# Attention and feed-forward layer on one core: the product of exponentials and values in two visits per group, three score banks, two max banks

## The reference, cut to what matters

```python
x: (16, 512, 128)
qkv = x @ c_attn_w + c_attn_b                       # 16 heads of 8
scores = einsum('bhqd,bhkd->bhqk', q, k) / sqrt(8)  # causal mask, softmax over k
out = einsum('bhqk,bhkd->bhqd', softmax(scores), v)
x = layernorm(x + out @ c_proj_w + c_proj_b)
h = relu(s0 * ([x, -x] @ W0)) * 2                   # 256 -> 512
h = relu(s1 * (h @ W1)) * 2                         # 512 -> 512
x = layernorm(x + s2 * (h @ W2))                    # 512 -> 128
```

## Time and profile before

| | |
|---|---|
| median of three runs | 1046.66 us (1042.14 to 1053.75) |
| the profiled execution's own time | 1043.98 us |
| its span in the profile | 1042.0 us |
| PE busy | 918.4 us, 88% |
| DVE busy | 673.2 us, 65% |
| ACT busy | 605.2 us, 58% |
| POOL busy | 439.5 us, 42% |
| mean granted PE clock | 0.934 of full |

### The profile page before, as it was taken

One profiled execution on the slowest core, in us unless ns is written; L12 is line 12 of the kernel. 1 busy time (PEld: TensorE's weight loads), 2 busy tenths in 40 slices (PEclk: granted clock), 3 DMA queues, 4 the chain that ended last, 5 costly groups with the idle time before them and its releaser, 6 DMA issues.

```text
span 1042.0 us, 20945 instructions
## 1 busy us (share of the span) xinstructions
PE 918.4 (88%) x6848; PEld 505.8 (49%) x6848; DVE 673.2 (65%) x1752; ACT 605.2 (58%) x1106; POOL 439.5 (42%) x505
## 2 busy tenths in 40 slices
PE   2449799999999799988999799998999999999865
PEld 1125345546555355644555355554546555555343
DVE  2346568695858468683776648685695858686334
ACT  2106467575757367573666647674675757566833
POOL 1103244544454345543354434543554454536440
PEclk9657899999999899997999889998999999999997
DMA  3653635354434415353253514534054534400000
GB/s 76 63 66 57 74 51 67 39 76 48 68 57 58 59 23 74 42 74 41 40 73 42 76 32 58 67 47 70 19 74 45 69 45 68 48 22 2 22 10 11
DMA packets 66157, 53.45 MB, mean 51 GB/s; under 512 B 4518, under 2 KB 64006, under 8 KB 66054
## 3 DMA queue, kind: packets, MB, share of 16 engines
q1 hardware_dynamic: 65190, 51.30, 37.4%
q10 hardware_dynamic: 864, 0.79, 0.3%
HBM read 9.24 MB, written 4.19 MB: 13 GB/s over the span
## 4 chain that ended last, share of the span: by engine, by line
PE 58%; ACT 13%; issue 10%; DVE 9%; DMA 5%; SPq 2%; ACTq 2%; POOL 1%; DVEq 0%; POOLq 0%
PE av_ps L899 10%; PE max_ps L840 9%; PE score_ps L866 9%; PE bank_ps L926 7%; PE bank_ps L927 6%; PE bank_ps L823 4%; ACT e L536 4%; ACT res L554 4%; PE max_ps L842 3%; PE bank_ps L972 3%; DMA stack<-parts 2%; DMA stack<-negmaxT 2%; ACT full L528 2%; PE bank_ps L961 2%; SPq L330 2%
## 5 line engine op out<-in xcount | busy, mean ns | idle before, releaser
L536 ACT ACTIVATE e<-score_ps 128x512 f32<-128x512 f32 x640 | 371.3, 598 | 245.2 <-PE score_ps L866 244.3
L840 PE MATMUL max_ps<-stack 72*128 72x512 bf16 (+3 forms) x1024 | 282.0, 315 | 54.7 <-DMA stack<-parts 26.0
L866 PE MATMUL score_ps<-stack 75*128 75x512 bf16 (+3 forms) x1024 | 251.7, 308 | 24.3 <-DMA stack<-negmaxT 15.8
L661 DVE TENSOR_REDUCE negmax<-max_ps 128x1 f32<-128x512 f32 x256 | 170.1, 684 | 155.6 <-PE max_ps L842 132.3
L445 POOL TENSOR_SCALAR_AFFINE_SELECT e<-e 128x512 f32<-128x512 f32 x256 | 164.1, 661 | 168.0 <-ACT e L536 168.0
L840 PEld LDWEIGHTS max_ps<-stack 72*128 72x128 bf16 x1024 | 102.2, 100 | 223.0 <-issue 85.8
L452 POOL TENSOR_TENSOR h_lo<-full,h_hi 128x512 fp32r<-128x512 f32 x120 | 155.3, 1299 | 120.5 <-DVE h_hi L741 119.8
L842 PE MATMUL max_ps<-ident_bf,future_bf 128*128 128x128 bf16 x1024 | 199.6, 227 | 0.0
L899 PE MATMUL av_ps<-e,vaug 128*9 128x512 f32 (+3 forms) x2048 | 193.5, 451 | 1.8 <-ACT avT L543 1.7
L664 DVE TENSOR_REDUCE negmax<-max_ps 128x1 f32<-128x384 f32 x256 | 140.1, 547 | 53.5 <-PE max_ps L842 53.1
L528 ACT ACTIVATE full<-bank_ps,scales 128x512 f32<-128x512 f32 x128 | 86.7, 689 | 101.7 <-PE bank_ps L927 100.0
(11 more groups left out here) (86 smaller groups left out, 950.6 us busy)
## 6 DMA issues: line engine op xcount, KB each, us to landing
stack<-parts SPq DMA_DIRECT2D x288, 128.0 KB
x_in<-in_L_attn_hidden_states SPq DMA_DIRECT2D x16, 256.0 KB, 4.2
x_res<-in_L_attn_hidden_states SPq DMA_DIRECT2D x16, 256.0 KB, 10.2
out_x<-res SPq DMA_DIRECT2D x16, 256.0 KB, 10.0
stack<-negmaxT ACTq DMA_DIRECT2D x32, 24.0 KB
e<-in_L_ffn_k SPq DMA_DIRECT2D x1, 256.0 KB, 3.3
wc<-in_L_attn_c_attn_w SPq DMA_DIRECT2D x1, 192.0 KB
e<-in_L_ffn_k SPq DMA_DIRECT2D x1, 128.0 KB, 3.2
```

What stands on the lines that cost most here:

```text
L536: nc.scalar.activation(e[g % 2][:, t, :], score_ps[:, t % 2, :], ACT.Exp, scale=SCALE).then_inc(exped, 1)
L661: ins = nc.vector.reduce_max(negmax[:, half, 3, h + t:h + t + 1], buf, AX.X, negate=True)
L840: nc.tensor.matmul(out_ap[:, col:col + width], st[0:QK_ROWS, h, 0, P * qt:P * qt + P], st[0:QK_ROWS, h, 1, 0:width], start=True, stop=False)
L866: return nc.tensor.matmul(out_ap[:, col:col + width], st[0:ALL_ROWS, h, 1, P * kt:P * kt + P], st[0:ALL_ROWS, h, 0, P * kt:S], start=True, ...
```

## The change

`SUM_STEPS = (1, 3, 5, 7)` becomes `SUM_STEPS = (2, 6)`: the product is made in two visits per group. The visit in step 2 takes kt 0 and kt 3, the one in step 6 takes kt 1 and kt 2. The first now waits for the second mask of its group, the second for the third. The same matmuls are made. The score ring grows from two banks to three, and the max ring shrinks from three banks to two, so that eight banks are still used. Since the score ring now runs over the 40 steps of a batch and 40 is not a multiple of three, the first step of a batch uses the bank of the step just before it.

```diff
-SUM_STEPS = (1, 3, 5, 7)
+SUM_STEPS = (2, 6)
+SUM_TILES = ((0, 3), (1, 2))
...
-    MAX_RING = 3
+    MAX_RING, SCORE_RING = 2, 3
...
-        score_ps = ctx.enter_context(nc.psum_tensor("score_ps", [P, 2, S], F32))
+        score_ps = ctx.enter_context(nc.psum_tensor("score_ps", [P, SCORE_RING, S], F32))
...
-                nc.scalar.activation(e[g % 2][:, t, :], score_ps[:, t % 2, :], ACT.Exp,
+                nc.scalar.activation(e[g % 2][:, t, :], score_ps[:, (STEPS * g + t) % SCORE_RING, :], ACT.Exp,
                                      scale=SCALE).then_inc(exped, 1)
...
             def scores(n, g, t):
-                st, out_ap = stack[n.parity], score_ps[:, t % 2, :]
+                i = STEPS * g + t
+                st, out_ap = stack[n.parity], score_ps[:, i % SCORE_RING, :]
...
-                if not (n.reg is None and n.c == 0 and g == 0 and t < 2):
-                    pe.wait_ge(exped, n.times(G * STEPS, STEPS * g + t - 1))
+                last_use = i - SCORE_RING
+                if i < SCORE_RING:
+                    last_use = max(j - G * STEPS for j in range(G * STEPS) if j % SCORE_RING == i)
+                if not (n.reg is None and n.c == 0 and last_use < 0):
+                    pe.wait_ge(exped, n.times(G * STEPS, last_use + 1))
...
-            def sums(b, g, kt, order):
-
-                if order == 0:
-                    pe.wait_ge(masked, b.times(3 * G, 3 * g + 1))
+            def sums(b, g, visit):
+
+                if visit == 0:
+                    pe.wait_ge(masked, b.times(3 * G, 3 * g + 2))
                     if g == 0:
                         pe.wait_ge(v_ready, b.times(1, 1))
                     if not (b.reg is None and b.c == 0 and g == 0):
                         pe.wait_ge(av_out, b.times(G, g))
-                elif order == 1:
-                    pe.wait_ge(masked, b.times(3 * G, 3 * g + 2))
-                elif order == 3:
+                else:
                     pe.wait_ge(masked, b.times(3 * G, 3 * g + 3))
...
+                for kt in SUM_TILES[visit]:
+                    for j in range(G):
...
+                        last = nc.tensor.matmul(av_ps[32 * j:32 * j + R + 1, P * kt:S],
+                                                vaug[b.parity][:, kt, G * g + j, :], src,
+                                                start=(kt == 0), stop=(kt == 2))
+                if visit == 1:
                     last.then_inc(summed, 1)
```

More of the change, by code:

```diff
@@ L885, in sums @@
                         pe.wait_ge(av_out, b.times(G, g))
-                elif order == 1:
-                    pe.wait_ge(masked, b.times(3 * G, 3 * g + 2))
-                elif order == 3:
+                else:
                     pe.wait_ge(masked, b.times(3 * G, 3 * g + 3))
[L890 to L902, removed]
+                for kt in SUM_TILES[visit]:
+                    for j in range(G):
+                        if kt == 0:
+                            src = e[g % 2][:, j, :]
+                        elif kt == 1:
+                            src = e[g % 2][:, 4 + j, 0:3 * P]
+                        elif kt == 3:
+                            src = e[g % 2][:, 4 + j, 3 * P:S]
+                        else:
+                            src = e[g % 2][:, 8 + j // 2, 2 * P * (j % 2):2 * P * (j % 2) + 2 * P]
+                        last = nc.tensor.matmul(av_ps[32 * j:32 * j + R + 1, P * kt:S],
+                                                vaug[b.parity][:, kt, G * g + j, :], src,
+                                                start=(kt == 0), stop=(kt == 2))
+                if visit == 1:
                     last.then_inc(summed, 1)
@@ L1004, in iteration @@
                         if t in SUM_STEPS:
-                            order = SUM_STEPS.index(t)
-                            kt = (0, 1, 3, 2)[order]
                             if g == 0 and live(n + -1):
-                                sums(n + -1, 3, kt, order)
+                                sums(n + -1, 3, SUM_STEPS.index(t))
                             if g > 0 and live(n):
-                                sums(n, g - 1, kt, order)
+                                sums(n, g - 1, SUM_STEPS.index(t))
                         fill(n, g, t)
```

## The result

The changed kernel takes 1177.19 us at the median (1171.09 to 1181.17), the kernel before 1046.56 us in the runs beside it: a ratio of 1.124 (95% interval 1.116 to 1.132), 131 us slower. The forecast was 1100 us with a range to 1130. The direction was right; the 56 us that were forecast are less than half of the 131.

What follows compares the result with a forecast made beforehand. PE's own stream was taken to set the pace. Waits of +79.8 us less 23.5 us of saved ways in and out gave +56.3 us on the profiled 1043.98 us, so 1100 us, range 1056 to 1130.

Steps and rivals of the forecast that it cites:

- Part 1: Fewer visits per group: each visit saved spares 0.21 us of getting in and out on PE, -23.5 us in all.
- Part 2: The third score bank: returns at most the 8.1 us of waits for exponentials; put at zero, 0 to -8 us.
- Part 3: Max ring of two: PE waits for VectorE's reductions two steps back, behind its side work; +79.8 us in the sum.
- A: Step (2, 6): PE waits 2.04 us for a reduction, starting 4.15 us after (2, 3); 26.5 us over 13 batches.
- B: Steps (2, 9) to (3, 2): PE waits 1.34 us, in two or three parts, behind VectorE's side work; 14 batches.
- C: Steps (0, 2) and (0, 3), start of a batch: 0.90 us lost, up to 1.8; 1.4 us taken, 14 batches.
- turns of the loop: Where the loop turns, VectorE comes back late: some 0.8 us more than C, four times, 3 us.
- R2: Rival: the clock drops too, one half-clock stretch of 3.4 us a batch, +24 us, 1124 us; chance 0.18.
- Place B2: Step (3, 5): PE waits for x1's low parts, no longer covered by the visits of steps 3 and 5; 0.6 us.
- R1: Rival: the saved drains win because VectorE's side work slips into PE's waits; 1020 us, faster; chance 0.06.
- R3: Rival: small waits only, 1048 to 1077 us; chance 0.18 for the part above 1054.
- R4: Rival: waits and drains cancel, no measurable change, 1036 to 1054 us; chance 0.06.

Runs made afterwards that it cites:

- the filler: The changed kernel with useless matmuls in front of the max-bank waits of steps (0, 2), (2, 6) and (2, 9): 1144.92 us, ratio 1.098.
- e2: The changed kernel's two visits per group alone, with the old rings (three max banks, two score banks): 1092.28 us, ratio 1.048 to the kernel before.
- e3: The changed kernel with the product of the max pass put behind scores and visit in each step: 1107.7 us, ratio 1.062 to the kernel before.
- e5: e2 with VectorE's last splitting of the maxima (L688) moved one step ahead, from (1, 2) to (1, 1): 1071.9 us, ratio 1.026.
- e1: The kernel before, its four visits kept, with the new rings alone (two max banks, three score banks): 1088.65 us, ratio 1.043.
- e13: The changed kernel with the filler and with L688 moved from step (1, 2) to (1, 1): 1119.46 us, ratio 1.068 to the kernel before.

## Why the prediction was right in its kind and wrong in its size

**In short.** The forecast of 1100 us fell 77 us short. Two terms that it put at nothing hold 58 of them: the half clock behind the new waits, for which the sum had no term (the filler gives back 32 us), and L688, which now falls into GpSimd's subtraction and which no term held (17 us). Both edits together give 58. A third step, the 23.5 us of saved ways in and out counted whole, is put in doubt by the kernels with three visits.

**What bounds the kernel.** Right: PE's stream, with room for VectorE only because of the third bank and the spread of the visits.

**Part 1, the ways in and out.** The price held: a visit of 640 columns takes 919.03 - 917.84 = 1.19 us to what follows, where 0.12 + 5 x 0.21 = 1.17 was forecast, so nothing is paid for changing from one kt to the next inside a visit. What failed is "I count it whole, since PE is the pace". The three kernels with three visits got 6 us or less of 13.4. The likely reason is that a shorter PE stream meets VectorE's and ScalarE's chains sooner.

**Part 2, the third score bank.** Near enough: forecast 0 to 8 us and put at zero in the sum, measured 10. Waits for exponentials fell from 8.1 to 1.9 us.

**Part 3, the max ring of two.** Places A, B and C are where the forecast put them. A has the forecast's length. B and C are 0.6 and 0.7 us longer in the batch read, where the clock had fallen. The wait in C is 1.86 us where 0.9 to 1.8 were thought possible and 1.4 taken. PE's waits for reductions grew to 101 us where some 60 were named as the sign; that figure was too small by my own sum, which has 80 us of waits, 71 of them for reductions. The turns of the loop were undersized: 2.2 us each, where the two waits read grew by 3.1 and 3.9.

**The term that was missing, half clock.** The forecast took its sum at full clock and gave the clock 24 us in rival R2, as one stretch of 3.4 us a batch. The batch read has two of 6.8 us; over 14 batches the rise of 133 us is 9.5 us of half clock a batch. Keeping PE busy in three waits gave back 32 us. R2's mechanism is what happened; its chance (0.18) and its price were both too low. In the first stretch of the earlier trace rows PE was idle for 3.40 - 1.70 = 1.70 us in all before the clock fell. The waits that I computed (2.04, 1.34 and 1.4 us) are near that, and I should have put the drop into the likeliest case once I had three of them in a batch.

**The other missing term, L688.** I gave step (1, 6) 0.25 us, said that VectorE's work would be unchanged, and did not follow DVE's queue behind the visit of (1, 2). Moving a visit in front of the transposes delayed the normalisation and with it L688, into POOL's subtraction. It costs 17 us in the change and 20 in e2.

**Place B2** (a wait for the low parts of x1) is there as forecast in kind: PE's wait for them is 9.6 us in all after the change and 2.0 before, where 14 x 0.6 = 8.4 were forecast.

**The masks.** Right: 1.0 us of wait in the change. They show where the cover is gone: 11.5 us in e3, 5.0 in e2, 8.6 in e5.

**The rivals.** R1 (the drains win), R3 and R4 fell. R3's lower bound took 36 us as what the ring of two costs where the visits stay; e1 is that kernel and lost 42 us, so this part was nearly right. But the saving of 23.5 us that R3 took off it did not come: the visits alone, e2, cost 46 us more.

With clock and L688 mended, e13 stands at 1119 us. So even without the two missing terms the forecast of 1100 was some 20 us low. At most 8 us of that are half clock. How much of the rest is the credit of 23.5 us taken whole, the undersized turns of the loop, or the filler's own time, the runs do not separate.

## What to carry to other kernels

A ring that gives a waiting engine less room is priced by the longest block of side work between two of the other engine's releases, and the work that stood in front of the wait must be counted as cover that leaves: here 3.40 us became 4.15 with 1.93 of idling. When a reckoning yields idle stretches on TensorE about as long as what the trace shows in front of a half-clock stretch, put the half clock into the sum. And when a long piece is moved in front of something that another engine waits for, follow that engine's whole queue to its end, also for what it will then run beside.

## What the runs showed of the hardware

Useless matmuls in front of three waits made a kernel faster by 32 us of 1177, because the granted clock stayed up (mean 0.924 in place of 0.885). A VectorE subtraction of 128 x 32 numbers took 1.85 us in place of 0.18 while GpSimd subtracted 128 x 1024, and ended with it. Going from the full array to four column tiles of 32 took 0.09 us (0.31 us from start to start in place of 0.22), and leaving them about 0.12 us beside 0.21 us for each 128 columns. Within a visit the next tile of keys, with new weights, cost nothing that shows: 640 columns took 1.19 us where this sum gives 1.17.
